# Local attention layers: the value product with its operands exchanged, the outputs turned afterwards, the output product at the end of the slot

## The reference, cut to what matters

```python
def local_attention(q, k, v):          # each window of 32 queries sees its own
    bk2, bv2 = (look(bk), look(bv))    # 32 keys and the 32 before them
    sim = jnp.einsum('bhwie,bhwje->bhwij', bq, bk2) * QK_SCALE
    sim = jnp.where(mask, -jnp.finfo(sim.dtype).max, sim)
    attn = jax.nn.softmax(sim, -1)
    out = jnp.einsum('bhwij,bhwje->bhwie', attn, bv2)
    return out.reshape(b, h, n, d)
...
for i in range(DEPTH):
    x = attn_layer(shift_tokens(x), Wqkv[i], q_scale[i], k_scale[i], Wo[i]) + x
    x = ffn_layer(shift_tokens(x), ln_g[i], ln_b[i], W1[i], b1[i], W2[i], b2[i]) + x
```

## Time and profile before

| | us |
|---|---|
| median of 3 runs | 3339.07 (3337.61 to 3339.78) |
| the profiled execution, its own time | 3358.94 |
| its span | 3357.2 |
| first to last add_back (L1571), 96 of them | 961.5 to 2763.2 in the span |
| PE busy | 2897.5 (86%) |
| DVE busy | 2017.1 (60%) |
| mean granted TensorE clock | 0.872 |

### The profile page before, as it was taken

The page is one execution under the profiler, slowest core; times in us unless marked ns, Lnnn a source line. Parts: engine busy times, 40 slices in busy tenths (PEclk is TensorE's granted clock), DMA queues, the critical chain, the costliest instruction groups (busy, mean ns, idle before and its releaser), DMA issues. The chain is left out here.

```text
span 3357.2 us, 91947 instructions
## 1 busy us (share of the span) xinstructions
PE 2897.5 (86%) x38047; PEld 1997.3 (59%) x38047; DVE 2017.1 (60%) x4601; ACT 1456.4 (43%) x2671; POOL 1461.3 (44%) x1324
## 2 busy tenths in 40 slices
PE   5779999997588898888888888888888886999987
PEld 1259999997355565555655555555555552545444
DVE  6822222221387887878878878878878763534314
ACT  4622332222155555555555555555555542233323
POOL 0053444432265656555655656565555531111111
PEclk9968988885599999999999999999999997567677
DMA  0000000000211111212222121112111110000000
GB/s 29 0 6 1 1 1 1 1 1 16 92 48 45 42 53 50 69 40 62 56 57 59 40 68 52 52 45 74 40 46 42 38 40 12 1 1 1 1 4 20
DMA packets 60615, 109.80 MB, mean 33 GB/s; under 512 B 14366, under 2 KB 18734, under 8 KB 59438
## 3 DMA queue, kind: packets, MB, share of 16 engines
q1 hardware_dynamic: 59280, 102.69, 10.9%
q10 hardware_dynamic: 926, 1.27, 0.1%
HBM read 28.93 MB, written 1.05 MB: 9 GB/s over the span
## 5 line engine op out<-in xcount | busy, mean ns | idle before, releaser
L1707 POOL TENSOR_TENSOR l_rot_a<-l_rot_a,l_rot_b 128x512 f32<-128x512 f32 x384 | 485.0, 1271 | 247.6 <-DVE l_rot_b L1523 245.4
L1716 POOL TENSOR_TENSOR l_qk<-l_rot_a,l_rn 128x512 f32<-128x512 f32 x384 | 388.3, 1042 | 426.2 <-DVEq L1566 410.1
L1169 PE MATMUL l_A<-l_wts,l_H 128*128 128x512 f32 x768 | 394.4, 611 | 29.7 <-ACT l_H L1466 21.7
L1259 PE MATMUL l_T<-ident,l_qk 128*128 128x128 f32 x1536 | 230.6, 296 | 131.9 <-ACT l_qT L1423 129.8
L1392 ACT ACTIVATE l_sq<-l_A 128x512 f32<-128x512 f32 x384 | 231.2, 602 | 227.3 <-PE l_A L1169 227.3
L1517 DVE TENSOR_TENSOR l_rot_a<-l_A,l_tab 128x512 f32<-128x512 f32 x384 | 263.1, 685 | 91.2 <-ACT l_sq L1392 84.6
L1259 PEld LDWEIGHTS l_T<-ident,l_qk 128*128 128x128 f32 x1536 | 178.8, 150 | 218.4 <-issue 209.0
L1523 DVE TENSOR_TENSOR l_rot_b<-l_A,l_tab 128x512 f32<-128x512 f32 x384 | 260.8, 679 | 0.0
L1527 DVE TENSOR_REDUCE l_ss<-l_sq 128x8 f32<-128x512 f32 x384 | 259.0, 674 | 0.0
L1244 PEld LDWEIGHTS l_O<-l_pT,l_vw 64*64 64x64 f32 x9216 | 196.9, 138 | 89.7 <-ACT l_pT L1398 83.3
L1990 ACT ACTIVATE a_pT<-a_t 128x384 f32<-128x384 f32 (+1 forms) x256 | 110.9, 462 | 261.7 <-PE a_t L1888 261.5
(11 more groups left out here) (336 smaller groups left out, 6202.4 us busy)
## 6 DMA issues: line engine op xcount, KB each, us to landing
l_vw<-l_vn SPq DMA_DIRECT2D x384, 128.0 KB
l_vw<-l_vn SPq DMA_DIRECT2D x360, 64.0 KB
l_wts<-in_l_wts SPq DMA_DIRECT2D x18, 650.0 KB, 5.5
l_tab<-in_l_tables SPq DMA_DIRECT2D x6, 1024.0 KB, 5.1
l_wts<-in_l_wts SPq DMA_DIRECT2D x6, 635.5 KB, 4.2
result<-x SPq DMA_DIRECT2D x4, 256.0 KB, 2.3
d_w_qkv<-in_d_w_qkv SPq DMA_DIRECT2D x1, 864.0 KB
l_scales<-in_l_scales SPq DMA_DIRECT2D x6, 128.0 KB, 5.9
```

The lines of the kernel that those rows point to most:

```text
L1169: pe.matmul(A[j % 2][:], cols(m), w_of(m)[:, C_QKV + 512 * j:C_QKV + 512 * j + 512], start=True, stop=True).then_inc(pq_done, 1)
L1259: last = pe.transpose(T[c % 2][:, P * i:P * i + P], qk[:, c, P * i:P * i + P], ident[:])
L1707: pool.tensor_tensor(rot_a[m % 2][:, j, :], rot_a[m % 2][:, j, :], rot_b[:, j, :], ALU.add).then_inc(rot_rdy, 1)
L1716: pool.tensor_tensor(qk[:, j, :].rearrange("p (a d) -> p a d", d=DH), rot_a[p][:, j, :].rearrange("p (a d) -> p a d", d=DH), rn[p][:, 8 * ...
```

## The change

The value product exchanges its operands: the turned probabilities (64 keys by 32 queries) are the weights, and the values (64 by 64) are moved past them. The result stands with queries in partitions, each head of a pair in its own bank O[e]. ACT copies it to a new tile `l_oS` (`keep_outputs`, where `keep_oT` stood), PE turns it in eight transposes (`turn_outputs`) into the T banks behind the turned keys, and ACT copies it to `l_oT` (`keep_oT`, now behind the turned keys). `project_v` moves ahead of the turning of the keys on PE, and `keep_v` ahead of their copies on ACT. The output product moves to the very end of the slot, behind the group work and `project(n + 3, 0)`. The rows of Wo are laid out anew on the host to fit. DVE, POOL and SP keep their programs.

```diff
@@ def values(m):
                 if n == TILES:
-                    pe.wait_ge(oT_rdy, 2 * m)
+                    pe.wait_ge(oS_rdy, 2 * m)
...
-                for i in range(4):
+                for pair in range(HP):
                     for wd in range(NWIN):
-                        for bank in range(2):
-                            for e in range(2):
-                                pair, half = 4 * bank + i, e ^ bank
-                                r = slice(DH * e, DH * e + DH)
...
-                                last = pe.matmul(O[bank][DH * half:DH * half + DH, P * i + WIN * wd:P * i + WIN * wd + WIN], keys,
-                                                 pT[r, pair, WIN * wd:WIN * wd + WIN], start=True, stop=True,
-                                                 skip_group_check=True)
+                        for e in range(2):
+                            r = slice(DH * e, DH * e + DH)
...
+                            last = pe.matmul(O[e][WIN * wd:WIN * wd + WIN, DH * pair:DH * pair + DH],
+                                             pT[r, pair, WIN * wd:WIN * wd + WIN], keys, start=True, stop=True,
+                                             skip_group_check=True)
                 last.then_inc(pv_done, 1)
+
+            def turn_outputs(m):
+                pe.wait_ge(oS_rdy, 2 * m + 2)
+                for half in range(2):
+                    if m + 2 < TILES:
+                        pe.wait_ge(qkT_rdy, 4 * (m + 2) + half + 3)
+                    else:
+                        pe.wait_ge(pT_rdy, 2 * m + half + 1)
+                    for i in range(4):
+                        last = pe.transpose(T[half][:, P * i:P * i + P], oS[:, half, P * i:P * i + P], ident[:])
+                    last.then_inc(oT_done, 1)
@@ the loop of PE
                 if has(n + 1):
+                    project_v(n + 1)
                     turn_qk(n + 1, 2)
                     turn_qk(n + 1, 3)
-                    project_v(n + 1)
                 if has(n - 1):
-                    output(n - 1)
+                    turn_outputs(n - 1)
                 if group_at(n, 0) is not None:
                     group_in(n, group_at(n, 0))
...
                 if has(n + 3):
                     project(n + 3, 0)
+                if has(n - 1):
+                    output(n - 1)
@@ scalar
-            def keep_oT(m):
+            def keep_outputs(m):
                 act.wait_ge(pv_done, m + 1)
                 if m >= 1:
+                    act.wait_ge(oT_done, 2 * m)
+                for e in range(2):
+                    act.activation(oS[:, e, :], O[e][:], ACT.Copy).then_inc(oS_rdy, 1)
+
+            def keep_oT(m):
+                if m >= 1:
                     act.wait_ge(y_done, m)
-                for bank in range(2):
-                    act.activation(oT[:, 4 * bank:4 * bank + 4, :].rearrange("p a q -> p (a q)"), O[bank][:], ACT.Copy).then_inc(oT_rdy, 1)
+                for half in range(2):
+                    act.wait_ge(oT_done, 2 * m + half + 1)
+                    act.activation(oT[:, 4 * half:4 * half + 4, :].rearrange("p a q -> p (a q)"), T[half][:], ACT.Copy).then_inc(oT_rdy, 1)
```

More of the change, by code:

```diff
@@ L1046, in local_layers @@
         pT = sb("l_pT", [P, HP, P])
+        oS = sb("l_oS", [P, 2, 512])
         oT = sb("l_oT", [P, HP, P])
@@ L1075, in local_layers @@
         v_done, v_rdy, vw_rdy = (sem("l_" + s) for s in ("v_done", "v_rdy", "vw_rdy"))
-        pT_done, pT_rdy, pv_done, oT_rdy, y_done, h_rdy = (sem("l_" + s) for s in (
-            "pT_done", "pT_rdy", "pv_done", "oT_rdy", "y_done", "h_rdy"))
+        pT_done, pT_rdy, pv_done, oS_rdy, oT_done, oT_rdy, y_done, h_rdy = (sem("l_" + s) for s in (
+            "pT_done", "pT_rdy", "pv_done", "oS_rdy", "oT_done", "oT_rdy", "y_done", "h_rdy"))
         x_done, x_rdy, st_rdy, mv_rdy, var_rdy, xn_rdy, xnT_done, xnT_rdy = (sem("l_" + s) for s in (
@@ L1174, in project_v @@
                     if m >= 2:
-                        pe.wait_ge(oT_rdy, 2 * (m - 2) + e + 1)
+                        pe.wait_ge(oS_rdy, 2 * (m - 2) + e + 1)
                     elif m == 1:
@@ L1209, in turn_probs @@
                         pe.wait_ge(h_rdy, m)
-                elif m + 1 < TILES:
-                    pe.wait_ge(qkT_rdy, 4 * (m + 1) + 4)
+                elif m >= 1:
+                    pe.wait_ge(oT_rdy, 2 * m)
+                else:
+                    pe.wait_ge(qkT_rdy, 8)
                 for i in range(4):
@@ L1233, in values @@
                     pe.wait_ge(back_rdy, group_at(n, 5) - (GROUPS - 4) + 1)
-                for i in range(4):
+                for pair in range(HP):
                     for wd in range(NWIN):
-                        for bank in range(2):
-                            for e in range(2):
-                                pair, half = 4 * bank + i, e ^ bank
-                                r = slice(DH * e, DH * e + DH)
[L1240 to L1243, removed]
-                                last = pe.matmul(O[bank][DH * half:DH * half + DH, P * i + WIN * wd:P * i + WIN * wd + WIN], keys,
-                                                 pT[r, pair, WIN * wd:WIN * wd + WIN], start=True, stop=True,
-                                                 skip_group_check=True)
-                last.then_inc(pv_done, 1)
+                        for e in range(2):
+                            r = slice(DH * e, DH * e + DH)
+                            if (wd, e) == (1, 0) or (wd, e) == (3, 1):
+                                keys = vn[p][r, e, DH * pair:DH * pair + DH]
+                            else:
+                                keys = vw[p][r, wd, DH * pair:DH * pair + DH]
+                            last = pe.matmul(O[e][WIN * wd:WIN * wd + WIN, DH * pair:DH * pair + DH],
+                                             pT[r, pair, WIN * wd:WIN * wd + WIN], keys, start=True, stop=True,
+                                             skip_group_check=True)
+                last.then_inc(pv_done, 1)
+            def turn_outputs(m):
[3 more added lines that the diff above has]
+                        pe.wait_ge(qkT_rdy, 4 * (m + 2) + half + 3)
+                    else:
+                        pe.wait_ge(pT_rdy, 2 * m + half + 1)
+                    for i in range(4):
+                        last = pe.transpose(T[half][:, P * i:P * i + P], oS[:, half, P * i:P * i + P], ident[:])
+                    last.then_inc(oT_done, 1)
             def turn_qk(m, c):
@@ L1263, in output @@
                 pe.wait_ge(oT_rdy, 2 * m + 2)
[L1264 to L1270, removed]
+                for two in range(HP):
+                    last = pe.matmul(T[0][:, 0:P], w_of(m)[:, C_WO + D * two:C_WO + D * two + D], oT[:, two, :],
+                                     start=(two == 0), stop=(two == HP - 1))
                 last.then_inc(y_done, 1)
@@ L1277, in bank_free @@
                 else:
-                    pe.wait_ge(oT_rdy, 2 * min(n, TILES) - 1 + bank)
+                    pe.wait_ge(oS_rdy, 2 * min(n, TILES) - 1 + bank)
             def group_in(n, k):
@@ L1292, in turn_norm @@
                 pe.wait_ge(v_rdy, 2 * min(n, TILES - 1) + 1)
-                pe.wait_ge(oT_rdy, 2 * min(n - 1, TILES))
+                pe.wait_ge(oS_rdy, 2 * min(n - 1, TILES))
                 for i in range(GT):
@@ L1484, in _ @@
                 if has(n - 1):
-                    keep_oT(n - 1)
+                    keep_outputs(n - 1)
                 if has(n + 1):
@@ L1491, in _ @@
                 if has(n + 1):
+                    keep_v(n + 1)
                     keep_qkT(n + 1, 2)
                     keep_qkT(n + 1, 3)
-                    keep_v(n + 1)
+                if has(n - 1):
+                    keep_oT(n - 1)
                 if group_at(n, 0) is not None:
@@ L1788, in pack_local_weights @@
     wts[:, :, C_V:C_WO] = Wqkv[:, :, 2 * INNER:].reshape(DEPTH, P, HP, 2, DH).transpose(0, 1, 3, 2, 4).reshape(DEPTH, P, INNER)
-    Wo = Wo.reshape(DEPTH, HP, 2, DH, D).copy()
-    Wo[:, HP // 2:] = Wo[:, HP // 2:, ::-1]
+    Wo = Wo.reshape(DEPTH, HP, 2, DH, D).transpose(0, 2, 1, 3, 4)
     wts[:, :, C_WO:C_W1] = Wo.reshape(DEPTH, HP, P, D).transpose(0, 2, 1, 3).reshape(DEPTH, P, HP * D)
```

## The result

| | before | changed |
|---|---|---|
| median | 3339.43 us (3337.61 to 3343.4, 4 runs) | 3622.36 us (3611.05 to 3639.44, 4 runs) |
| ratio | | 1.0854 (95% interval 1.0806 to 1.0902) |
| span of the profiled execution | 3357.2 us | 3617.4 us |
| first to last add_back | 1801.7 us | 2080.2 us |

The changed kernel is 8.5% slower. The forecast was 3627 us. The local stretch, read from the first to the last add_back, grew by 278.5 us. The parts on either side of it account for little: the first add_back comes 19.5 us earlier than in the trace of before, and the end of the span comes 595.2 instead of 594.0 us after the last.

A forecast was written before the change was run, and what follows sets the result against it. The prediction took the loop DVE, ACT, PE, DVE through the output product to bound the kernel. It added 238 us of later add_back and 50 us of clock to 3339, giving 3627 us, range 3550 to 3715.

The forecast's parts named there:

- The loop is the bound: DVE, ACT, PE, DVE from one add_back to the next, 18.13 us, bounds the kernel; chance with moderate clock toll 0.83.
- The value product counted at nothing: On PE, 2.00 to 1.41 us a slot, ahead of a wait for ACT: counted 0, bounds 0 and -57 us.
- The new tail: From ACT's output copy to the next add_back: 8.00, 8.32 or 9.60 us by kind of slot, against 6.36.
- The split of the 238 us: Later add_back: 156 us over 95 rounds, plus 8 us for group_in and 74 us for two gates or linears.
- The clock, 50 us: Longer PE idle lowers the granted clock in the local stretch: 50 us taken, between 0 and 116.
- the three idle stretches: PE idle grows to 3.6 us before narrow, 3.1 before turn_norm, about 3.2 before the values' projection after the gates.
- The wait before the turned outputs: PE waits about 0.7 us a slot before turn_outputs for ACT's copy of the turned keys, newly added.
- The slow clock: Rival: PE's clock stays at the lower level through much of the slot, time near 3840 us; chance 0.08.
- PE's work had been the bound: Rival: the output product's place does not matter, PE's work does; +33 us, so 3372 us; chance 0.06.
- The faster side: Rival: values' projection fills the 3.73 us gap, ending slow clock there; 39 us won, 3300 us; chance 0.03.
- the share of the weight loads: Skill's measure for TensorE; by it, halving the value product's weight columns should gain; no size given.

The follow-up runs named there:

- the move alone: Kernel before with only the output product moved to the end of the slot, behind the group work and the projection of tile n+3; 3585.17 us, ratio 1.0702.
- the filled one: Changed kernel with 24 idle PE transposes added ahead of narrow and 24 ahead of turn_norm; 3559.59 us, ratio to before 1.0650.
- the interleaved kernel: Kernel before with the halves of the values' projection and the two key turnings alternating on PE, ACT's copies reordered to match; 3266.81 us, ratio 0.9753.

## Why the prediction was right, and where it was off

- *The loop is the bound.* Shown from both sides. The same PE work in an order that shortens the loop took 67 us off the stretch. Work taken from PE without shortening the loop gave nothing (0.9976). A projection and the group work moved ahead of the output product cost 253 us of the stretch. Work added to PE outside the loop made two kernels faster.
- *The value product counted at nothing.* 1.46 us where 1.41 was taken from the scores. With the exchange alone more than half of the gain went into the wait behind it, and the time did not move beyond its interval.
- *The new tail.* 9.60 at full clock in the linears slot, as summed, step by step within 0.1 us. In the kinds where the product itself waits for its copy the shortest tails are 8.09 and not 8.00: behind a wait the step from product to add_back is 2.09 and not 1.99. That term was too small by 0.1 us.
- *The split of the 238 us.* 82 us for the group work and 156 for the rest. The run with the product moved back took 110 off the stretch, the 82 and some 30 of clock, and left 169.
- *The clock, 50 us.* This term was too small. Two of the three idle stretches came nearly as worked out: 3.57 before narrow where 3.6 was expected, and 3.37 before turn_norm where 3.1 was, as this line of the timeline of the changed kernel shows:

```profile
1665.67 0.66 PE L1303 MATMUL l_O<-ident,l_xn 128*128 128x128 f32 x4 [3.37 <-ACT l_xn L1467]
```

The third was mis-sized. In the slot that follows the gates about 3.2 us were expected before the values' projection, and at most 2.11 were there: that projection is due 0.96 earlier, and the head is 0.72 shorter (next point), and the sum of the idle stretches took neither off. Even so 7 of the 22 tails of this kind ran 10.84 to 10.99 instead of 9.60. Two such slots, the idle being the same:

```profile
1250.19 1.98 PE L1179 MATMUL l_O<-l_wts,l_H 128*128 128x512 f32 x4 [2.11 <-ACT l_oS L1419]
```

```profile
2320.55 2.82 PE L1179 MATMUL l_O<-l_wts,l_H 128*128 128x512 f32 x4 [2.10 <-ACT l_oS L1419]
```

Filling the first two stretches gave 62 us, 12 more than I had allowed for all of the toll, and the fill leaves part of it in place. By difference, from the table: 12.1 us a group, less 10.1 of the sum and 0.1 of the wait behind the copies, plus the 0.7 of the next point, leaves some 2.6 us a group for the clock, about 60 us.
- *What stood against it.* In the linears slot the head fell from 11.76 us in most rounds to 11.04 in all, by 0.72, 17 us in 23 groups, which the prediction did not have. Before, ACT loads the table of the exponential behind a square, and the load ended after the scores' shift:

```profile
1538.83 1.22 DVE L1536 TENSOR_TENSOR l_sd<-l_S,l_mx 128x1024 f32<-128x1024 f32 x1
...
1539.50 1.28 ACT L1402 ACT_TABLE_LOAD   x1
1540.79 1.06 ACT L1402 ACTIVATE l_sd<-l_sd 128x1024 f32<-128x1024 f32 x1
```

In the changed kernel PE's work in that slot starts earlier with respect to add_back, the square too, and the load is over before the shift:

```profile
1600.15 1.28 ACT L1412 ACT_TABLE_LOAD   x1
...
1602.04 1.22 DVE L1555 TENSOR_TENSOR l_sd<-l_S,l_mx 128x1024 f32<-128x1024 f32 x1
...
1603.29 1.06 ACT L1412 ACTIVATE l_sd<-l_sd 128x1024 f32<-128x1024 f32 x1 [1.86 <-DVE l_sd L1555]
```

It comes with the output product's place and with nothing else: the head of this slot is 11.04 in both other kernels that have the product at the end (the move alone, the filled one), and 11.76 again in the one with the product moved back and in the one with the values first.
- *How near the number came.* 3622 against 3627 is in part luck. The tails were right, within 0.1 us a round, but the clock took some 10 us more than its term and the table load gave 17 back; the two errors have opposite signs.
- *The wait before the turned outputs.* 0.65 in the slot shown, 0.7 expected. In rounds where PE is late it is shorter: 35.3 us in 79 waits.
- *The rivals.* The slow clock did not hold through the slots: the shortest tails of all four kinds lie within 0.2 us of the sums at full clock, and what the lower clock cost is some 60 us, not 200 or more. If PE's work had been the bound, the changed kernel had come out at 3372, and the exchange alone 57 us below the kernel before; neither is so. The faster side fell with the tails: in the 88 rounds of the table none is shorter than 8.09, and the share of the weight loads, by which that reading went, fell from 59% to 56% of the span while the time went up. An output product that starts earlier than 4.37 behind O does exist, at 3.46 in the interleaved kernel and at 4.14 with the values first alone, but not with the turned outputs ahead of it.

## What to carry to other kernels

Find the wait that ends every round, follow the round back to itself, and price an edit by where it stands in that loop; an engine at 86% was not the bound, and its 57 us of saved work were worth nothing that could be measured. A step whose result closes the loop goes as soon as its input is ready, and work that nobody in the loop waits for goes behind it. Before an operation is moved, look also at what it covered, such as the copy out of a bank that the next product writes.

## What the runs showed of the hardware that I had not expected

Idle PE cost more than extra PE work. Repeating a projection three times, 2.6 us of useless work in every fourth slot, made the kernel before 41 us faster over the stretch, since the work behind the wait then ran at full clock in all 22 rounds of that kind. The Trainium skill, "TensorE: Matmul & The Clock Gate", section "HAM oscillation — how this bites in real kernels", advises to arrange the work so that the engine stays at the fast level; these runs agree, and show that filler does it too.

Idle stretches of 2.1 to 2.6 us did not decide the matter by their length. Of the two in the earlier trace rows, 2.34 was followed by eight transposes at a granted clock of 1.00, and 2.33 by the same at 0.50, 1.2 GHz. Of the two slots of the changed kernel shown above, 2.11 was followed by work at 1.00 and a tail of 9.61, and 2.10 by work at 0.65 on the mean and a tail of 10.90. In the run with the move alone, 2.58 before the turned keys of that slot was followed by a tail of 9.90 in one round and of 11.30 to 11.39 in six others. What tells these rounds apart stays open.
